# A four-layer kernel on one core: layer 0's modulations by column tiles, biases off TensorE, fused weights moved, y's first half taken later by ScalarE

## The chip, the cores and the metric

The kernel runs on one core of a Trainium2 chip. The metric is the device time of one execution in microseconds; lower is better. Before the change the median of three executions is 1902.47 us (1902.10 to 1903.45).

## The reference

Two sequences (2 x 1024 tokens x 256 channels, float32) go through four layers that are modulated by a vector of 512 numbers each. Cut to what matters:

```python
# layer 0: linear attention, 8 heads
xn = _ln(x, ln_w, ln_b)
q = softmax((xn @ Wq + bq).reshape(b, t, h, dh), axis=-1)
k = softmax((xn @ Wk + bk + mask).reshape(b, t, h, dh), axis=1)
v = ((xn @ Wv + bv) * src_mask).reshape(b, t, h, dh)
y = q @ (k^T v)                               # per head
scale, shift = split(silu(emb) @ W_emb + b_emb)
x = x + silu(_ln(y) * (1 + scale) + shift) @ W_out + b_out
# layer 1: tokens permuted, a Mamba block with 512 channels, 16 states
shift, scale, gate = split(silu(c) @ W_ada + b_ada)
h = (_layernorm(x) * (1 + scale) + shift)[:, perm]
def step(hst, inp):
    dA = exp(dt_t[:, :, None] * A)
    hst = hst * dA + (dt_t * x_t)[:, :, None] * B_t[:, None, :]
    y = einsum('bds,bs->bd', hst, C_t)
x = x + gate * ((y + xm * D) * silu(z) @ W_out)[:, inv_perm]
# layer 2: two such scans, forward and over the flipped sequence
mz = _ln(x_ssm) @ Wz.T + bz
z1 = _ssm(mz @ Wc1.T + bc1, ...);  z2 = flip(_ssm(flip(mz @ Wc2.T + bc2), ...))
out = (silu(mx) * z1 + silu(mx) * z2) @ Wf.T + bf + skip
# layer 3: softmax attention, 16 heads, then a modulated output as in layer 0
```

## The kernel before

**One program per engine.** Each engine runs a list of instructions written out in its own order (functions ending in `_sp` for SyncE, which starts the transfers, `_p` for GpSimd, `_t` for TensorE, `_s` for ScalarE, `_v` for VectorE). `w.wait_ge` makes an engine wait for a semaphore's value, and the instruction waits in order: what stands behind it on the engine waits too. `up(key)` names an event, `at(key)` is what others wait for. The eight PSUM banks are handed out in a ring: `take` waits until the bank's last reader has called `banks.give`.

**Layer 0** goes over 16 tiles of 128 tokens, in pairs. `first_t` projects q and v of a tile into one bank (bias matmul of three bf16 rows at line 440, two k-steps at 442) and transposes exp(k) (448). `first_s` copies v and exp(k) out, `first_v` reduces each q head's maximum (573), subtracts it and, one pair later, sums and normalises. Then TensorE forms attention (458), y, and between these the modulations: silu(c) times a weight matrix. `column_mods_t` (284) does that for values needed along partitions, as 16 accumulated narrow products with one or two columns, `row_mods_t` (320) for values needed along rows. Transposes (243) and the output projection (265) end it. The middle of layer 1's head gathers permuted rows from memory.

**Fused weights.** Layer 2 needs only Wz.Wc1 and Wz.Wc2 with their biases Wc.bz. `fuse_t(n)` makes both halves m = 0, 1 of matrix n (1069) and its bias (1074); it stands in the inputs of run one (n = 0) and of run two (n = 1). `fuse_s` (1080) copies the halves out. SyncE loads the second matrix after the first has been fused, `wzc1`, ahead of the C rows of run one in its queue.

**Six runs of scans.** A run is one sequence through one selective scan (layer 1, sequence 0 and 1; then layer 2, forward and backward for each sequence). `run_t`, `run_s`, `run_v`, `run_p` and `run_sp` work it off together. A run has 128 units: (half of 512 tokens) x (16 states) x (4 blocks of 128 channels). For a unit ScalarE makes the decay exp(dt A) (945), TensorE forms u = dt x B in PSUM three units ahead (854 with a diagonal of B that ScalarE spreads, 929, or 860 by transposing what ScalarE scaled, 922), VectorE scans (1014), ScalarE keeps the carry for the second half (937). GpSimd multiplies two units at once by a row of C that SyncE has loaded into all partitions (1037, loads at 815). TensorE adds these products up in four PSUM banks, transposed back to tokens (879). After 64 units the first half's y must be taken out of these banks before the second half's first product can be added. `take_s` and `take_v` do that, one bank of four each:

```python
        def by_scalar(r, p, j):
            return r.n < 2 and (p == 0 or j >= 2)
```

So in the runs with r.n = 0 or 1 (one, two, three and five) ScalarE takes the whole first half, and the last two banks of the second. In the backward ones (r.n = 2: four and six) VectorE takes all and adds it to the forward y (832). The take stands at unit `TAKEN_AT` = 71. At a run's end `turn_back_t` (1047) transposes y to channels, `turn_back_v` (1054) multiplies by the gates; in backward runs `open_gates_s` (1298), a SILU over 2 x 2048 elements, makes these gates just before, given to `run_s` as `early`. The start of a run (`inputs_t` and others, 672 and 691) prepares what the units need: ScalarE scales transposed inputs (749) and copies them (753), VectorE forms dt x (786).

## Time and profile before

| | before |
|---|---|
| median of three executions | 1902.47 us |
| profiled execution | 1901.27 us |
| its span (first to last instruction) | 1899.5 us |
| TensorE matmuls busy | 1816.6 us, 96% |
| VectorE busy | 1593.3 us, 84% |
| ScalarE busy | 1427.9 us, 75% |
| GpSimd busy | 1091.9 us, 57% |
| mean granted TensorE clock | 0.987 |

The busy shares are means over stages with different limits. The runs take from about 195 to 1399 us of the span; a little under 200 us lie before them and 500 behind (layer 3 mostly). A row of a timeline gives its start, the time to its end, engine, line, operation, output and inputs with shapes, and how many instructions it holds; in brackets stands the idle time of the engine before it and whose event ended it.

### The profile page before, as it was taken

To read this page: it belongs to the slowest core of one execution; us is meant where nothing else is said; L and a number is where in the kernel's file an instruction comes from. 1 tells how busy PE (TensorE), PEld (TensorE's weight loads), DVE (VectorE), ACT (ScalarE), POOL (GpSimd) and SP (SyncE) were. 2 spreads that over 40 slices of the span, in tenths; PEclk is the share of its full clock that TensorE was granted. 3 is DMA by queue.
4 is the path that set the end of the run, shared out by engine and by line. 5 is a ranking of instruction groups with operands and counts; after the bars stand their busy time and mean duration, and the time that the engine had idled before them with its cause. 6 is when DMAs were issued, how large, how long until landed. Compare 5 with 4: busy or idle time off the path is not lost.

```text
span 1899.5 us, 32305 instructions
## 1 busy us (share of the span) xinstructions
PE 1816.6 (96%) x12120; PEld 1309.2 (69%) x12120; DVE 1593.3 (84%) x2109; ACT 1427.9 (75%) x2669; POOL 1091.9 (57%) x615
## 2 busy tenths in 40 slices
PE   7999899998999999999999999999999999999997
PEld 3664899848997599959985799789974333322333
DVE  6566899578998699989995999799988888898772
ACT  3426999369993899799973999799955677776665
POOL 3022799438994499949990799679955400003000
PEclk9989899999999999999999999999999999999998
DMA  5032211121111112101110111121101111111101
GB/s 207 1 114 76 67 57 59 43 65 38 59 57 38 48 58 59 53 24 57 56 45 2 40 57 57 30 67 57 59 21 38 38 28 37 33 38 28 33 18 42
DMA packets 57546, 95.16 MB, mean 50 GB/s; under 512 B 14951, under 2 KB 23559, under 8 KB 55982
## 3 DMA queue, kind: packets, MB, share of 16 engines
q1 hardware_dynamic: 55854, 88.90, 15.5%
q0 software_dynamic: 1536, 4.20, 0.7%
q8 instruction: 96, 1.57, 0.3%
q14 instruction: 60, 0.49, 0.1%
HBM read 73.55 MB, written 6.91 MB: 42 GB/s over the span
## 4 chain that ended last, share of the span: by engine, by line
PE 51%; POOL 21%; issue 11%; ACT 10%; DVE 6%; SPq 1%; DMA 0%; DVEq 0%; ACTq 0%; POOLq 0%
POOL A L1037 20%; PE PS L256 8%; PE PS L1622 6%; PE PS L1574 6%; PE PS L879 5%; PE PS L1781 5%; PE PS L854 4%; PE PS L265 4%; PE PS L860 2%; ACT A L945 2%; PE PS L442 2%; DVE A L1587 1%; ACT A L922 1%; PE PS L243 1%; PE PS L1456 1%
## 5 line engine op out<-in xcount | busy, mean ns | idle before, releaser
L1037 POOL TENSOR_TENSOR A<-A 128x1024 f32<-128x1024 f32 x384 | 896.2, 2397 | 39.6 <-DVE A L1014 25.8
L945 ACT ACTIVATE A<-A,negA 128x512 f32<-128x512 f32 x768 | 547.6, 716 | 33.7 <-DVE A L1014 23.9
L1014 DVE TENSOR_TENSOR_SCAN A<-A,PS 128x512 f32<-128x512 f32 x384 | 434.7, 1199 | 27.4 <-PE PS L860 16.2
L1014 DVE TENSOR_TENSOR_SCAN A<-A,small,PS 128x512 f32<-128x512 f32 x384 | 451.2, 1256 | 5.6 <-ACT A L945 5.6
L879 PE MATMUL PS<-ident,A 128*128 128x128 f32 x3072 | 408.5, 275 | 23.9 <-ACT A L753 13.4
L854 PE MATMUL PS<-A 128*128 128x128 f32 x3072 | 392.6, 277 | 1.5 <-ACT A L929 1.2
L879 PEld LDWEIGHTS PS<-ident,A 128*128 128x128 f32 x3072 | 351.7, 142 | 34.0 <-ACT A L753 15.8
L854 PEld LDWEIGHTS PS<-A 128*128 128x128 f32 x3072 | 368.8, 192 | 5.5 <-DVE A L1014 2.8
L1587 DVE TENSOR_REDUCE A<-PS 128x1 f32<-128x512 f32 x512 | 319.7, 680 | 38.9 <-PE PS L1574 37.6
L1816 ACT ACTIVATE A<-PS 128x512 f32<-128x512 f32 x512 | 269.2, 604 | 106.6 <-PE PS L1781 106.3
L922 ACT ACTIVATE A<-A,small 128x512 f32<-128x512 f32 x320 | 228.7, 715 | 7.3 <-PE PS L860 7.2
L860 PE MATMUL PS<-ident,A 128*128 128x128 f32 x1360 | 197.3, 278 | 6.4 <-ACT A L753 3.0
L256 PE MATMUL PS<-A,W 128*128 128x512 f32 (+1 forms) x416 | 184.9, 598 | 3.3 <-DVE A L780 2.9
L1781 PE MATMUL PS<-A 102*128 102x512 bf16 x480 | 178.9, 381 | 7.0 <-ACT A L1816 5.1
L1574 PE MATMUL PS<-A 99*128 99x512 bf16 x480 | 179.8, 382 | 4.2 <-DVE A L1587 2.7
L1552 POOL CAST W<-W 128x32 bf16<-128x32 f32 x32 | 6.7, 209 | 303.6 <-DVE W L1545 303.6
L860 PEld LDWEIGHTS PS<-ident,A 128*128 128x128 f32 x1360 | 158.1, 142 | 15.2 <-DVE A L1014 4.9
L230 POOL TENSOR_TENSOR RS<-VE,HALF 128x8 f32<-128x8 f32 (+1 forms) x15 | 26.8, 1785 | 214.9 <-DVE VE L225 214.8
L929 ACT ACTIVATE A<-ident,small 128x128 f32<-128x128 f32 x384 | 149.1, 395 | 0.8 <-PE PS L854 0.8
L1574 PEld LDWEIGHTS PS<-A 99*128 99x128 bf16 x480 | 46.6, 97 | 146.1 <-DVE A L1587 108.1
L256 PEld LDWEIGHTS PS<-A,W 128*128 128x128 f32 (+1 forms) x416 | 75.1, 185 | 102.7 <-issue 91.6
L1622 PE MATMUL PS<-A,W 128*32 128x512 f32 x1024 | 136.5, 604 | 0.0
(195 smaller groups left out, 1827.7 us busy)
## 6 DMA issues: line engine op xcount, KB each, us to landing
A<-scrc SPq DMA_DIRECT2D x192, 256.0 KB, 3.1
A<-A SPq DMA_DIRECT2D x360, 32.0 KB
scr<-A SPq DMA_DIRECT2D x4, 1024.0 KB, 5.2
W<-in_wa SPq DMA_DIRECT2D x2, 1536.0 KB, 10.6
X<-in_x SPq DMA_DIRECT2D x4, 512.0 KB, 5.5
scr<-W SPq DMA_DIRECT2D x128, 1.5 KB
out<-X SPq DMA_DIRECT2D x4, 512.0 KB, 3.0
W<-in_w SPq DMA_DIRECT2D x1, 1984.0 KB
```

The costliest lines, as they stand in the source:

```text
L256: t = e.matmul(o[0:M, :], wt(k, m), act_in(k), start=k == 0, stop=k == nk - 1)
L854: t = e.matmul(o[:, j * 128:(j + 1) * 128], r.DUT[:, 4 * ci + j, dt * 128:(dt + 1) * 128], DB[k // 2 % 2][:, j, :], start=True, stop=True)
L860: t = e.transpose(o[:, j * 128:(j + 1) * 128], r.G[(2 * k + j) % 6][:, dt * 128:(dt + 1) * 128], ident[:, :])
L879: t = e.matmul(PS[:, j, dt * 128:(dt + 1) * 128], r.H[pair % HS][:, dt % 2, j * 128:(j + 1) * 128], ident[:, :], start=open_y(ci, j), stop ...
L945: e.activation(A_B[i % 4], r.DT[:, dt, ci * 512:(ci + 1) * 512], ACT.Exp, scale=negA[:, r.n, dt * 16 + s:dt * 16 + s + 1]).then_inc(*decay ...
L1014: e.tensor_tensor_scan(h, a, u, init, ALU.mult, ALU.add).then_inc(*scanned.up((q, i)))
L1037: e.tensor_tensor(h, h, CB[k % 2].unsqueeze(1).broadcast_to([128, 2, 512]), ALU.mult).then_inc(*weighed.up((q, pair)))
L1574: e.matmul(o, SQ[j][0:99, nt * 128:(nt + 1) * 128], SK3[j][0:99, c * 512:(c + 1) * 512], start=True, stop=True).then_inc(*pe.up(("trial", ...
L1587: e.tensor_reduce(NM[:, k % 2, q:q + 1], bank(("trial", k, nt, c)), AX.X, ALU.max, negate=True).then_inc(*dve.up(("trial", k, nt, c)))
L1622: t = e.matmul(PV[32 * q:32 * q + 32, u % 2, :], V[:, tile * 272 + 17 * h:tile * 272 + 17 * h + 32], PX[mt % 4][j][:, c * 512:(c + 1) * 51 ...
L1781: e.matmul(o, SK3[sl][0:102, mt * 128:(mt + 1) * 128], SQ[sl][0:102, c * 512:(c + 1) * 512], start=True, stop=True).then_inc(*pe.up(("scor ...
L1816: e.activation(PX[mt % 4][j][:, c * 512:(c + 1) * 512], bank(key), ACT.Exp).then_inc(*act.up(("weights", u, mt, j, c)))
```

## The change

It does seven things. (1) The bias of q and v no longer is a matmul: SyncE loads it into all partitions (`bias_qv`), VectorE adds q's in an instruction per tile, GpSimd adds v's (times the mask) to the copied v. (2) Column and row modulations are formed as a 32-column stationary operand (silu(c) padded by zeros, `sc32`) against 512 columns of weights, the four k-blocks in four column tiles of the array. ScalarE copies the parts, and short matmuls with `sel` add the four blocks up. (3) The biases of the fused weights take the same way (`bias_parts_t`). (4) Three of the four fused products stand at the end of layer 0; the last stands in run one's inputs. SyncE loads these weights in `first_sp`, and nothing of them in `layer1_sp`. (5) ScalarE pulls two transposed inputs of the second half at units 6 and 7, not 9 and 10. (6) ScalarE takes y's first half at the point of unit 75 and not 72, in all runs, and TensorE forms u of one unit before it adds up there. (7) In backward runs ScalarE takes the first half, and banks 2 and 3 of the second, into a buffer of its own (`r.DUT`), and `turn_back_t` adds it by a second transpose into the same bank. Line numbers move: what stood at 1014 (scan), 1037 (GpSimd) and 945 (decay) now stands at 1101, 1124 and 1030.

```diff
+        def parts_t(e, w, key, lhs, rhs):
+
+            o = take(w, (key, "parts"))
+            for n, (at, wt) in enumerate(rhs):
                 for k in range(4):
-                    t = e.matmul(o[:, 2 * m:2 * m + 2], wt[:, k, at:at + 128], sc[:, k, :], start=k == 0, stop=k == 3)
-            t.then_inc(*pe.up(("mods", layer)))
+                    t = e.matmul(o[32 * k:32 * k + 32, at[0]:at[1]], lhs[:, k, :], wt(k), start=True, stop=True, tile_position=(0, 32 * k),
+                                 skip_group_check=True)
+            t.then_inc(*pe.up((key, "parts")))
+
+        def parts_s(e, w, key):
+            w.wait_ge(*pe.at((key, "parts")))
+            e.activation(parts_of(key), bank((key, "parts")), ACT.Copy).then_inc(*act.up((key, "parts")))
+            banks.give((key, "parts"), act.now())
+
+        def column_sums_t(e, w, key, chunks):
+            o = take(w, key)
+            w.wait_ge(*act.at((key, "parts")))
+            for m, at in chunks:
+                t = e.matmul(o[:, 2 * m:2 * m + 2], parts_of(key)[:, at:at + 128], sel, start=True, stop=True)
+            t.then_inc(*pe.up(key))
...
@@ first_p
+            for i in range(0, NT, 2):
+                w.wait_ge(*act.at(("v", i + 1)))
+                e.tensor_tensor(V0[:, i:i + 2, :], V0[:, i:i + 2, :], BVM[:, i:i + 2, :], ALU.add).then_inc(*pool.up(("v", i)))
@@ first_t, loop over pairs of tiles
-                    e.matmul(o, ones3[0:3, :], ROW3[0:3, 0:512], start=True, stop=False)
                     for k in range(2):
-                        t = e.matmul(o, XN[:, k, (i + j) * 128:(i + j + 1) * 128], w0[:, 0:3:2, k, :], start=False, stop=k == 1)
+                        t = e.matmul(o, XN[:, k, (i + j) * 128:(i + j + 1) * 128], w0[:, 0:3:2, k, :], start=k == 0, stop=k == 1)
@@ first_t, end
+            for n in range(2):
+                bias_parts_t(e, w, n)
+            for n in range(2):
+                row_sums_t(e, w, n)
+            column_sums_t(e, w, ("mods", 2), orders(2))
+            for n, m in FUSED[0:3]:
+                fuse_t(e, w, n, m)
+            for n in range(2):
+                column_sums_t(e, w, ("bzc", n), [(j, 128 * j) for j in range(4)])
@@ first_v
-                    e.tensor_reduce(m, b3, AX.X, ALU.max, negate=True).then_inc(*dve.up(("qmax", j)))
+                    e.tensor_tensor(Q0[:, j, :], bank(("qv", j))[:, 0:256], BQ, ALU.add).then_inc(*dve.up())
+                    banks.give(("qv", j), dve.now())
                     w.wait_ge(*dve.now())
-                    e.tensor_tensor(q3, b3, m.unsqueeze(2).broadcast_to([128, 8, 32]), ALU.add).then_inc(*dve.up(("qsub", j)))
-                    banks.give(("qv", j), dve.now())
+                    e.tensor_reduce(m, q3, AX.X, ALU.max, negate=True).then_inc(*dve.up(("qmax", j)))
+                    w.wait_ge(*dve.now())
+                    e.tensor_tensor(q3, q3, m.unsqueeze(2).broadcast_to([128, 8, 32]), ALU.add).then_inc(*dve.up(("qsub", j)))
@@ taking y
         def by_scalar(r, p, j):
-            return r.n < 2 and (p == 0 or j >= 2)
+            return p == 0 or j >= 2
+
+        def taken_to(r, p, j, y):
+
+            i = 4 * r.order[p] + j
+            return r.DUT[:, i, :] if r.n == 2 else y(i)
@@ run_t
-                if dt % 2 and i >= 7:
+                late = i == 2 * (PAIRS_N // 2) + 7
+                if dt % 2 and i >= 7 and not late:
                     add_up((i - 7) // 2)
                 form_u(i + 3)
+                if late:
+                    add_up((i - 7) // 2)
@@ run_s
+            if q == 0:
+                fuse_s(e, w, *FUSED[3])
             for j in range(4):
                 if not first_state(r, j)[2]:
                     scale_du_s(e, w, r, j)
...
-                if i == TAKEN_AT + 1:
+                if i == TAKEN_AT + 4:
...
-                if i in (9, 10):
-                    copy_du_s(e, w, r, 1, i - 7)
+                if i in (6, 7):
+                    copy_du_s(e, w, r, 1, i - 4)
@@ turn_back_t
-                    t = e.transpose(o[:, j * 128:(j + 1) * 128], y(4 * c + j)[:, m * 128:(m + 1) * 128], ident[:, :])
+                    parts = [y(4 * c + j)] + ([taken_to(r, p, j, y)] if r.n == 2 and by_scalar(r, p, j) else [])
+                    for n, part in enumerate(parts):
+                        t = e.matmul(o[:, j * 128:(j + 1) * 128], part[:, m * 128:(m + 1) * 128], ident[:, :], start=n == 0, stop=True,
+                                     is_transpose=True, skip_group_check=True)
@@ layer1_sp
             store_c_sp(e, w, runs[0])
-            w.wait_ge(*act.at(("wzc", 0)))
-            w.wait_ge(*dve.at(("bzc", 0)))
-            e.dma_start(w2all, T["wzc"][:, 3072:5120]).then_inc(*transfer("wzc1").up(0))
             run_sp(e, w, runs[0])
```

Three places show how the instructions move. A row gives line, operation, output and inputs by buffer name, size and count.

TensorE's queue at the end of layer 0, from the output projection of sequence 0 (265, now 267) on. Before, the modulations are narrow products (284) and row products (320):

```order
L265 MATMUL PS<-A 128x256 x16
L284 MATMUL PS<-sc,W 128x2 x16
L320 MATMUL PS<-W,sc 2x256 x4
L243 MATMUL PS<-ident,A 128x128 x16
L265 MATMUL PS<-A 128x256 x16
L320 MATMUL PS<-W,sc 2x256 x4
L320 MATMUL PS<-W,sc 2x512 x4
L284 MATMUL PS<-sc,A 128x2 x16
L243 MATMUL PS<-ident,A 128x128 x16
```

Now (293 are the column tiles, 309 and 348 the sums, 1167 the three fused products):

```order
L267 MATMUL PS<-A 128x256 x16
L293 MATMUL PS<-W,small 32x512 x4
L293 MATMUL PS<-A,small 32x512 x4
L245 MATMUL PS<-ident,A 128x128 x16
L309 MATMUL PS<-small,A 128x2 x4
L267 MATMUL PS<-A 128x256 x16
L293 MATMUL PS<-A 32x512 x8
L348 MATMUL PS<-A,small 2x512 x2
L309 MATMUL PS<-small,A 128x2 x4
L1167 MATMUL PS<-A 128x512 x12
L309 MATMUL PS<-small,A 128x2 x8
L245 MATMUL PS<-ident,A 128x128 x16
```

Between the second projection and layer 1's first transposes (243, now 245) stand the fused products now.

ScalarE's queue at the end of run four, before:

```order
L929 ACTIVATE A<-ident,small 128x128
L945 ACTIVATE A<-A,negA 128x512 x8
L1298 ACT_TABLE_LOAD
L1298 ACTIVATE A<-A 128x4x512 x2
L250 ACTIVATE A<-PS,COL 128x512 x4
```

And now:

```order
L1014 ACTIVATE A<-ident,small 128x128
L1030 ACTIVATE A<-A,negA 128x512 x8
L908 ACTIVATE A<-PS 128x512 x2
L1391 ACT_TABLE_LOAD
L1391 ACTIVATE A<-A 128x4x512 x2
L252 ACTIVATE A<-PS,COL 128x512 x4
```

Two copies of y's banks (908), which wait for the last addition, stand ahead of the gates (1391).

ScalarE's queue at the start of run one, from the first decays (945, now 1030), before and then now:

```order
L945 ACTIVATE A<-A,negA 128x512 x4
L749 ACTIVATE A<-PS,small 128x512 x4
L753 ACTIVATE A<-PS 128x512 x4
L929 ACTIVATE A<-ident,small 128x128 x4
L1080 ACTIVATE W<-PS 128x512 x2
L922 ACTIVATE A<-A,small 128x512
```

```order
L1030 ACTIVATE A<-A,negA 128x512 x4
L1172 ACTIVATE W<-PS 128x512
L826 ACTIVATE A<-PS,small 128x512 x4
L830 ACTIVATE A<-PS 128x512 x4
L1014 ACTIVATE A<-ident,small 128x128 x4
L1007 ACTIVATE A<-A,small 128x512
```

One copy of fused weights (1172) stands ahead of the scalings (826) in place of two (1080) behind the spreads.

## Rows read from the trace of the kernel before

**Rows 1.** Timeline of VectorE, middle of run one.

```profile
284.89 1.28 DVE L1014 TENSOR_TENSOR_SCAN A<-A,small,PS 128x512 f32<-128x512 f32 x1 [1.39 <-ACT A L945]
```

**Rows 2.** Timeline of GpSimd across the same moment.

```profile
267.78 23.37 POOL L1037 TENSOR_TENSOR A<-A 128x1024 f32<-128x1024 f32 x10
```

**Rows 3.** GpSimd's waits (us, count, longest), 436 to 590 and 841 to 990.

```profile
POOL A L1037 <- DVE A L1014: 5.3, 3, 4.2
...
POOL A L1037 <- DVE A L1014: 6.3, 3, 5.8
```

**Rows 4.** Timeline of TensorE, layer 0.

```profile
50.93 0.38 PE L440 MATMUL PS<-ROW,ones 3*128 3x512 bf16 x1
51.24 1.99 PE L442 MATMUL PS<-A 128*128 128x512 f32 x4
...
74.09 5.27 PE L458 MATMUL PS<-A 128*128 128x128 f32 x32
...
80.95 3.74 PE L458 MATMUL PS<-A 128*128 128x128 f32 x32
...
94.49 2.93 PE L243 MATMUL PS<-ident,A 128*128 128x128 f32 x16 [0.91 <-ACT negA L521]
...
98.58 7.17 PE L265 MATMUL PS<-A 128*128 128x256 f32 x32 [1.16 <-ACT A L250]
```

**Rows 5.** Timeline of VectorE, two tiles of layer 0's loop.

```profile
46.27 0.42 DVE L573 TENSOR_REDUCE small<-PS 128x8 f32<-128x256 f32 x1 [1.35 <-ACT A L504]
...
48.94 0.42 DVE L573 TENSOR_REDUCE small<-PS 128x8 f32<-128x256 f32 x1 [0.18 <-ACT A L504]
```

**Rows 6.** Groups by line, 0 to 215 us: busy us, mean ns, idle before.

```profile
L320 PE MATMUL PS<-W,sc 128*2 128x256 f32 (+1 forms) x24 | 8.9, 532 | 0.0
...
L284 PE MATMUL PS<-sc,W 128*128 128x2 f32 x64 | 8.5, 268 | 0.0
```

**Rows 7.** Timeline of TensorE, layer 3.

```profile
1500.64 1.07 PE L1622 MATMUL PS<-A,W 128*32 128x512 f32 x8
```

**Rows 8.** Timeline of TensorE, start of run one.

```profile
179.40 7.06 PE L1069 MATMUL PS<-W 128*128 128x512 f32 x16
186.30 3.63 PE L1074 MATMUL PS<-COL,W 128*128 128x2 f32 x32
```

**Rows 9.** Windows: PE, PEld, DVE, ACT, POOL busy (instructions), granted clock, DMA share, GB/s.

```profile
132.00:138.00 6.00, 6.00 (x23) 4.86 (x24) 4.15 (x19) 3.10 (x4) 0.51 (x1) 0.50 0.01 5
```

**Rows 10.** Timeline of ScalarE, start of run one.

```profile
190.92 0.69 ACT L749 ACTIVATE A<-PS,small 128x512 f32<-128x512 f32 x1 [3.55 <-PE PS L672]
...
197.09 1.10 ACT L1080 ACTIVATE W<-PS 128x512 f32<-128x512 f32 x2
```

**Rows 11.** Timeline of SyncE, loads of C's rows, start of run one.

```profile
198.59 15.19 SPq L815 DMA_DIRECT2D A<-scrc  x4
```

**Rows 12.** Timeline of GpSimd, start of run one.

```profile
204.13 11.62 POOL L1037 TENSOR_TENSOR A<-A 128x1024 f32<-128x1024 f32 x5 [8.93 <-ACT small L937]
```

**Rows 13.** Timeline of ScalarE, start of run two.

```profile
427.72 2.42 ACT L749 ACTIVATE A<-PS,small 128x512 f32<-128x512 f32 x4 [3.08 <-PE PS L672]
```

**Rows 14.** Timeline of VectorE, end of run four.

```profile
991.97 2.48 DVE L1054 TENSOR_TENSOR A<-PS,A 128x512 f32<-128x512 f32 x4 [1.86 <-PE PS L1047]
```

**Rows 15.** Timeline of ScalarE, end of run four.

```profile
986.20 1.28 ACT L1298 ACT_TABLE_LOAD   x1
987.49 3.71 ACT L1298 ACTIVATE A<-A 128x2048 f32<-128x2048 f32 x2
```

**Rows 16.** Timeline of TensorE, end of run four.

```profile
991.26 1.91 PE L1047 MATMUL PS<-ident,A 128*128 128x128 f32 x16
...
996.89 1.64 PE L1047 MATMUL PS<-ident,A 128*128 128x128 f32 x13 [0.27 <-DVE A L832]
```

**Rows 17.** Timeline of VectorE, start of run one.

```profile
178.74 2.29 DVE L786 TENSOR_TENSOR A<-A 128x2048 f32<-128x2048 f32 x1 [4.17 <-ACT A L720]
...
186.03 3.16 DVE L786 TENSOR_TENSOR A<-A 128x2048 f32<-128x2048 f32 x1
```

## What the change is predicted to do

> **What bounds the kernel now.** I read the page's slices first, then the timelines of single engines. The span has three kinds of stretch, and an edit is worth something only by the limit of its own stretch.
>
> Six runs of 64 pairs of scans. In the middle of the first run VectorE stands still for 1.39 us at the turn to the second half [rows 1], yet GpSimd's ten multiplications across that moment take 23.37 us with no pause, 2.34 us each [rows 2]. So GpSimd sets the pace from its first pair to its last; VectorE only has to stay ahead. A run ends when GpSimd has done 64 pairs, and gets shorter only by an earlier first pair or by fewer pauses of GpSimd. The waits of GpSimd on VectorE come to 5.3 us in the second run, of which 4.2 is the wait before the first pair, and to 6.3 with 5.8 before the first in the fourth [rows 3]: 1.1 and 0.5 us of pauses are left.
>
> Layer 0 and the head of layer 1 (to about 168 us). TensorE works nearly without a pause, and what it has to do is the time.
>
> Starts and ends of runs: chains of one engine after another.
>
> **The change, part by part.**
>
> 1. Biases of q and v off TensorE. The bias matmul takes 51.24 - 50.93 = 0.31 us of TensorE's time per tile [rows 4]; 16 tiles, 5.0 us. VectorE gets an addition per tile; its neighbours of that shape take 0.42 us, 0.46 with the dependency, 0.92 for a pair of tiles. It idles 1.35 + 0.18 = 1.53 us in each pair [rows 5], and a pair gets 0.62 shorter on TensorE: 1.53 - 0.92 - 0.62 is nothing, so VectorE goes from idle to level with TensorE. I count the whole 5.0 for TensorE, since banks let it run more than two pairs ahead. GpSimd's additions to v are needed only by the attention matmuls after the loop.
>
> 2. Column and row modulations by column tiles. Before: 64 narrow matmul instructions take 8.5 us, 0.133 each, so the three sets of 32 take 12.8; the row ones take 8.9 [rows 6]; together 21.7, of which I take 0.5 off because modelled ends overlap the next start: 21.2. After: a group of four column tiles, 512 wide, is 8 instructions and takes 1.0 us where the kernel already does that [rows 7]. Five groups are 5.0. Three column sums are 8 narrow instructions each, 0.95, so 2.85. Two row sums are 2 instructions of 512 columns each, at the 0.44 of the 16 wide ones in [rows 8]: 1.8. That is 9.7, so 11.5 saved. ScalarE's copies of the parts (0.6 each) fall where it idles.
>
> 3. Fusions. All of Wz.Wc was done at the starts of runs one and two: two products in 7.06 us and the bias in 3.63 [rows 8], in each. Now three of four products stand at the end of layer 0 (10.3 us) with both biases (2 groups, 2.0, and 16 narrow instructions, 1.8): 14.1 us added there. They could hide a wait for the gathered rows, but TensorE has had none there.
>
> 4. Clock. After the long stretches of narrow matmuls TensorE's granted clock is 0.50, its 1.2 GHz level [rows 9]. The first attention product takes 5.27 us at it and 3.74 as the second one at the full level [rows 4]: 1.5 lost. The 6 us at 132 to 138 [rows 9] do the work of 3: 3.0 lost. The narrow stretches shrink from 32 instructions to 8, so I expect both back, 4.5. Bounds: 0 and 4.5.
>
> TensorE also waits 0.91 before the transposes of normalised y and 1.16 before the output projection [rows 4]; parts now stand in these places: 2.0. Front: 5.0 + 11.5 - 14.1 + 4.5 + 2.0 = **8.9 us** earlier at the first run. Bounds 3 and 10.
>
> 5. Start of run one. TensorE fuses until 189.8, while ScalarE idles 3.55 us for the transposed inputs; two copies of fused weights (1.0 us) come later [rows 8, 10]. Left: one product (3.5 us), hidden behind VectorE's input of run one, and one copy, placed ahead. ScalarE: 3.55, about 0.5 of small waits between the four scalings (an estimate), and 1.0 for the copies less 0.6 for the one that stays: 4.5 earlier. But GpSimd's first pair waits longer than ScalarE explains: SyncE issues the first row of C at 198.59 only, behind the load of the second half of the weights, which waits for that fusion [rows 11], and GpSimd starts at 204.13 [rows 12]. That load is gone from the queue, so the pair can start after ScalarE's first carry, which comes about a pair's work of ScalarE earlier; I take 2.2 for it, just under GpSimd's pace of 2.34 [rows 2]: 204.1 - 2.2 - 4.5 = 197.4. **6.7 us**. Bounds: 4.5 and 6.9.
>
> 6. Start of run two. ScalarE's wait of 3.08 us for the transposes [rows 13] goes, and its two copies (1.0): 4.0. VectorE is then the next to be late. The two pulls of inputs moved from units 9 and 10 to 6 and 7 end TensorE's waits in units 9 to 13, and with them the 1.1 us of GpSimd's pauses: **5.1**. Bounds 3 and 6. Runs four and six: 0.5 each, **1.0**. Runs three and five have no such pause: 0.
>
> 7. y's first half three units later. VectorE's 1.39 us vanish in four runs, and four additions (2.48 us, the shape of the gatings in [rows 14]) in two. GpSimd never stopped there [rows 2], so I count **0**; the cover is its lead of about one pair of work. If the cover were gone: 4 x 1.4 + 2 x 2.5 = 10.6 us.
>
> 8. Backward y. ScalarE now takes y tiles 2 and 3 at the end of runs four and six, and `run_s` puts these copies ahead of `open_gates_s`, which was free to run before the end. Before: the table load at 986.20 and the two SILUs are done by 991.2 [rows 15]; VectorE's four gatings start at 991.97 [rows 14]. After, in the times of that run: the last 32 transposes of the first half (16 before, 1.91 us with its modelled end [rows 16], some 1.75 from start to start) take 3.5 us, 991.26 to 994.76; the last addition (0.62 as a gating [rows 14], with its hand-overs) 1.0, 995.8; ScalarE's two copies of the last bank, 996.6; table load 1.28, 997.9; first SILU 1.86, 999.8 [rows 15]; four gatings 2.48, 1002.2; VectorE's two copies, then TensorE's 24 transposes. Before, the fourth addition let TensorE go at 996.89 with 13 transposes left, 1.6 us [rows 16], so it ended at 998.5. Now VectorE's second addition is done at 1003.5, 22 or 23 transposes are left, 2.7 us: 1006.2. **7.7 us** later, and the output projection stands behind it in TensorE's queue. Twice: **+15.4**. Bounds 6 and 8.5 for each. This is the largest single term.
>
> Sum: -8.9 - 6.7 - 5.1 - 1.0 + 15.4 = -6.3 on the profiled execution's 1901.3, 1895.0; the median of the runs is 1.2 above that execution, so **1896 us**.
>
> **Two rules against the change.** VectorE's product over 2048 elements takes 2.29 us alone and 3.16 while GpSimd multiplies [rows 17]. In the loop of layer 0 GpSimd will add v's bias while VectorE subtracts and normalises; VectorE has no slack there by step 1. If each pair of tiles loses 0.9 us so, eight pairs lose 7, of which TensorE's lead of some two pairs hides a part: the front gives 4 in place of 8.9. The Trainium skill (SBUF - State Buffer, on the shared port pair) says that a VectorE instruction with two SBUF inputs and a GpSimd instruction that reads SBUF shut each other out for the whole instruction; by that rule the trace agrees, and the sum would be near 1901.
>
> The groups of four column tiles take 1.0 us between other matmuls [rows 7], so a switch costs little. The Trainium skill (TensorEngine Tiling (Array Packing), Key Properties) says that changing the tiling mode drains TensorE; no row prices the drain apart.
>
> **Rivals.**
> - The late gate is right, the front gives less (the lock above, the low clock staying, or the gathered rows late by what TensorE gained): 4 to 6 us of the 8.9 gone, 1900 to 1902, no change. For: VectorE has no slack. Against: the attention products come later. 0.20.
> - VectorE, not GpSimd, is the pace after all, so step 7 pays 10: 1886. Against it: [rows 2]. 0.08.
> - The gate costs nothing (the SILUs are hidden): 1881. It would need ScalarE to open gates before its copies, and the order says no. 0.04.
> - Slower: GpSimd's first pair in runs one and two hangs on VectorE's second input product and its own scaling of the skip, and not on ScalarE or the row of C. Then steps 5 and 6 give 0 to 2 of 11.8 and the late gates decide: 1906. It decides from the point at which less than 6 of the 11.8 come. Against it: GpSimd idles 8.93 us before the first pair [rows 12]. 0.06.
> - Forecast: 1892 to 1900, 0.62.
>
> **Numbers.** About 0.2% (3.8 us) is what a measurement of this kernel can tell from no change, so faster means under 1898.7. Of the forecast's 0.62 about four fifths lie there; with 0.08 and 0.04 and some of the first rival, faster 0.66. Same: the rest of the forecast and most of the first rival, 0.27. Slower 0.07. The range, 1888 to 1902, leaves out the fast rivals and the slow one.
>
> **What would show it.** Per tile 1.9 us on TensorE in layer 0's loop; groups of 8 instructions at 1.0; no half clock before 190 us; the first conv projection some 9 us earlier; GpSimd's first pair near 188 in run one; VectorE's pause in mid-run gone, GpSimd's row unchanged; and at the end of runs four and six a table load after the last addition, with VectorE idle some 8 us before its gatings. Wrong if that idle time is absent, if GpSimd pauses in mid-run, or if a wait for gathered rows stands before the first transposes of layer 1.

## The result

The changed kernel takes 1911.42 us (median of 7 executions, 1909.74 to 1915.74) where the kernel before took 1902.11 (7 executions, 1898.73 to 1903.45). The ratio is 1.0057, 95% interval 1.0044 to 1.007: slower by 9 us between the medians, outside the predicted range and on the other side of no change. The profiled execution of the changed kernel takes 1915.28 us with a span of 1913.4, 13.9 longer than the span before; it is one of three executions near 1915, at a granted clock of 0.983, while the other four lie between 1909.7 and 1911.4 at 0.985 to 0.986.

The busy times of the page hardly explain that. TensorE does less and is granted less of its clock (0.983, 0.987 before):

```profile
PE 1803.4 (94%) x12076; PEld 1299.4 (68%) x12076; DVE 1601.0 (84%) x2114; ACT 1435.6 (75%) x2688; POOL 1110.8 (58%) x627
```

What explains it is a list of milestones, read from the timelines of TensorE and GpSimd of the two profiled executions (us). A part of the change is what its stretch gains or loses between two of them.

| milestone | before | after | after - before | this stretch | predicted |
|---|---|---|---|---|---|
| first attention product, layer 0 | 74.09 | 63.90 | -10.2 | -10.2 | |
| first projection, layer 1 | 136.32 | 134.61 | -1.7 | +8.5 | -8.9 for both |
| GpSimd's last pair ends, run one | 354.00 | 345.00 | -9.0 | -7.3 | -6.7 |
| the same, run two | 589.40 | 577.91 | -11.5 | -2.5 | -5.1 |
| the same, run three | 808.85 | 798.38 | -10.5 | +1.0 | 0 |
| the same, run four | 992.60 | 981.47 | -11.1 | -0.7 | -0.5 |
| first output projection after run four | 998.67 | 999.36 | +0.7 | +11.8 | +7.7 |
| GpSimd's last pair ends, run five | 1215.05 | 1216.85 | +1.8 | +1.1 | 0 |
| the same, run six | 1398.86 | 1399.95 | +1.1 | -0.7 | -0.5 |
| first output projection after run six | 1404.90 | 1417.98 | +13.1 | +12.0 | +7.7 |
| end of the span | 1899.49 | 1913.38 | +13.9 | +0.8 | 0 |

**Layer 0.** TensorE goes through the loop faster than was predicted. A pair of tiles took 4.90 us from start to start:

```profile
55.82 0.39 PE L440 MATMUL PS<-ROW,ones 3*128 3x512 bf16 x1
...
60.72 0.38 PE L440 MATMUL PS<-ROW,ones 3*128 3x512 bf16 x1
```

It takes 3.87 now (the prediction takes 0.62 off a pair, the rows show 1.03):

```profile
55.35 3.60 PE L486 MATMUL PS<-A 128*128 128x512 f32 x8
...
59.22 3.60 PE L486 MATMUL PS<-A 128*128 128x512 f32 x8
```

So TensorE comes 10.2 us earlier to attention, and gives 8.7 of it back within 21 us. Its timeline from the last of layer 0's loop on:

```profile
63.90 3.82 PE L507 MATMUL PS<-A 128*128 128x128 f32 x32
67.56 1.40 PE L515 MATMUL PS<-ident,A 128*128 128x128 f32 x8
69.19 0.66 PE L515 MATMUL PS<-ident,A 128*128 128x128 f32 x4 [0.24 <-DVE A L647]
70.99 0.66 PE L515 MATMUL PS<-ident,A 128*128 128x128 f32 x4 [1.14 <-DVE A L647]
74.29 3.78 PE L507 MATMUL PS<-A 128*128 128x128 f32 x16 [2.64 <-ACT A L572]
79.38 3.78 PE L507 MATMUL PS<-A 128*128 128x128 f32 x16 [1.31 <-DVE MT L317]
...
134.61 31.14 PE L258 MATMUL PS<-A,W 128*128 128x512 f32 x72 [0.35 <-issue]
```

Where the second attention product had no wait before it and took 3.74 us [rows 4], it stands in two halves now, each of 3.78 us behind a wait; TensorE's granted clock is at the half level from 72.9 to 83.1 us. VectorE has no idle time at all from 40 to 58 us and is the one that is late. Its timeline shows one instruction twice as long for every other tile, and four much too long at the end:

```profile
64.87 0.98 DVE L652 TENSOR_TENSOR A<-A,small 128x256 f32<-128x256 f32 x1
...
66.67 0.42 DVE L652 TENSOR_TENSOR A<-A,small 128x256 f32<-128x256 f32 x1
...
71.42 1.66 DVE L652 TENSOR_TENSOR A<-A,small 128x256 f32<-128x256 f32 x1
...
74.00 1.84 DVE L664 TENSOR_TENSOR A<-A,small 128x512 f32<-128x512 f32 x1
...
76.97 1.65 DVE L664 TENSOR_TENSOR A<-A,small 128x512 f32<-128x512 f32 x1
...
79.35 1.49 DVE L320 TENSOR_SCALAR MT<-MT 128x4 f32<-128x4 f32 x1
```

GpSimd's timeline has the counterpart: an addition to v beside the first, and from 70.28 on four additions of the output bias to x. Those stood at 21 us before; they have been queued behind the additions to v.

```profile
64.30 1.27 POOL L459 TENSOR_TENSOR A<-A 128x512 f32<-128x512 f32 x1 [3.49 <-ACT A L567]
69.05 1.27 POOL L459 TENSOR_TENSOR A<-A 128x512 f32<-128x512 f32 x1 [3.48 <-ACT A L567]
70.28 10.54 POOL L463 TENSOR_TENSOR X<-X,A 128x1024 f32<-128x1024 f32 x4
```

**The runs.** GpSimd's first pair of run one starts at 194.35 where it started at 204.13 [rows 12], and then GpSimd has a pause that it did not have, between its first and its second pair:

```profile
194.35 2.37 POOL L1124 TENSOR_TENSOR A<-A 128x1024 f32<-128x1024 f32 x1 [1.92 <-issue]
198.25 2.37 POOL L1124 TENSOR_TENSOR A<-A 128x1024 f32<-128x1024 f32 x1 [1.53 <-ACT small L1022]
```

It stands in all six runs, 1.5 to 1.7 us in four and 0.8 in the backward ones, and waits for the carry (1022). In mid-run nothing has changed for GpSimd, as in [rows 2]: eleven pairs in 25.69 us, 2.34 each.

```profile
261.16 25.69 POOL L1124 TENSOR_TENSOR A<-A 128x1024 f32<-128x1024 f32 x11
```

VectorE's pause there has not gone, as was predicted, but shrunk from 1.39 to 0.82 us, and it waits for TensorE's addition now; runs four and six, which had none, have the same 0.82.

```profile
276.28 9.55 DVE L1101 TENSOR_TENSOR_SCAN A<-A,small,PS 128x512 f32<-128x512 f32 x8 [0.82 <-PE PS L961]
```

**The ends of runs four and six** are the largest loss. TensorE, then VectorE, then ScalarE, end of run four:

```profile
980.98 5.25 PE L1136 MATMUL PS<-ident,A 128*128 128x128 f32 x32
986.06 1.04 PE L961 MATMUL PS<-ident,A 128*128 128x128 f32 x8
994.61 4.61 PE L1136 MATMUL PS<-ident,A 128*128 128x128 f32 x24 [7.51 <-DVE A L914]
999.15 0.28 PE L194 MATMUL PS<-ROW,ones 3*128 3x256 bf16 x1
```

```profile
991.47 2.49 DVE L1144 TENSOR_TENSOR A<-PS,A 128x512 f32<-128x512 f32 x4 [15.49 <-ACT A L1391]
993.87 1.27 DVE L914 TENSOR_TENSOR A<-A,PS 128x512 f32<-128x512 f32 x2
```

```profile
987.13 1.08 ACT L908 ACTIVATE A<-PS 128x512 f32<-128x512 f32 x2 [15.08 <-PE PS L961]
988.24 1.28 ACT L1391 ACT_TABLE_LOAD   x1
989.53 3.71 ACT L1391 ACTIVATE A<-A 128x2048 f32<-128x2048 f32 x2
```

The reader sees the chain as predicted: last addition, two copies, table load, one SILU, four gatings, two additions of VectorE, 24 transposes. In the windows view (busy time and count of PE, PEld, DVE, ACT and POOL, then the granted clock) one also sees what the sum left out, a lowered clock. It is at the half level twice, from 977.4 to 984.2 us, which begins before the last pair ends and ahead of TensorE's long wait, and from 991.0 to 997.9, which begins in that wait:

```profile
978.00:986.00 8.00, 7.22 (x43) 6.82 (x42) 0.00 (x0) 0.00 (x0) 3.47 (x2) 0.61 0.00 0
986.00:994.00 8.00, 1.10 (x11) 0.86 (x8) 2.53 (x5) 6.08 (x5) 0.00 (x0) 0.82 0.00 0
994.00:1000.00 6.00, 5.27 (x28) 4.64 (x29) 3.93 (x7) 0.00 (x0) 0.00 (x0) 0.68 0.00 0
```

### The profile page after: what moved, and what is told of

It is laid out like the page before. It is cut to its first block, busy times and chain, and to the rows that moved or that the text cites. A ratio compares the mean times of both kernels' runs of the same rounds, so it can differ in the third digit from the quotient of the medians.

```text
span 1913.4 us, 32264 instructions
## 1 busy us (share of the span) xinstructions
PE 1803.4 (94%) x12076; PEld 1299.4 (68%) x12076; DVE 1601.0 (84%) x2114; ACT 1435.6 (75%) x2688; POOL 1110.8 (58%) x627
## 4 chain that ended last, share of the span: by engine, by line
PE 38%; ACT 27%; POOL 18%; issue 8%; DVE 7%; SPq 1%; DMA 0%; DVEq 0%; POOLq 0%; ACTq 0%
POOL A L1124 17%; ACT A L1030 12%; PE PS L258 8%; PE PS L1715 6%; PE PS L1667 6%; ACT A L1007 5%; PE PS L1874 5%; PE PS L267 4%; ACT A L1014 3%; DVE A L1680 1%; PE PS L1136 1%; ACT small L1022 1%; PE PS L245 1%; PE PS L749 1%; PE PS L1549 1%
## 5 line engine op out<-in xcount | busy, mean ns | idle before, releaser
L936 PE MATMUL PS<-A 128*128 128x128 f32 x3072 | 388.3, 276 | 0.3
L1014 ACT ACTIVATE A<-ident,small 128x128 f32<-128x128 f32 x384 | 150.1, 397 | 0.0
## 6 DMA issues: line engine op xcount, KB each, us to landing
W<-in_wa SPq DMA_DIRECT2D x2, 1536.0 KB, 10.5
```

The lines of the kernel that those rows point to most:

```text
L936: t = e.matmul(o[:, j * 128:(j + 1) * 128], r.DUT[:, 4 * ci + j, dt * 128:(dt + 1) * 128], DB[k // 2 % 2][:, j, :], start=True, stop=True)
```

## The experiments

Executions of one kernel differ by up to 6 us; so stretches of the profiled executions decide where single microseconds matter, and medians where the sum does. In what follows, "the stretch" is from the end of GpSimd's last pair to the first output projection's matmul with the weights, after run four and after run six. It is 6.1 and 6.0 us before the change, 17.9 and 18.0 after.

The clock moves this stretch too. Four of the kernels below leave that chain as the change has it: it takes 16.2 and 16.2 us (pulls at 9 and 10), 16.7 and 16.4 (no additions to v), 16.2 and 18.4 (additions to x first), 17.9 and 18.1 (biases on TensorE). Where it is 16.2 to 16.7 there is no half clock ahead of the wait, and the 32 transposes take 3.66 us, but the 24 behind it are slow all the same. TensorE at the end of run four, pulls at 9 and 10:

```profile
977.16 3.66 PE L1136 MATMUL PS<-ident,A 128*128 128x128 f32 x32
...
989.20 5.37 PE L1136 MATMUL PS<-ident,A 128*128 128x128 f32 x24 [7.51 <-DVE A L914]
```

### The gates ahead of the copies

```diff
-                run_s(e, w, two, y2, lambda part: gates_s(e, w, b, GATES[PARTS[part]]))
-                open_gates_s(e, w, b)
+                run_s(e, w, two, y2, lambda part: gates_s(e, w, b, GATES[PARTS[part]]), lambda: open_gates_s(e, w, b))
```

> The changed kernel, with ScalarE's opening of the gates placed ahead of its last two copies of y in runs four and six; all else as changed. Measured on the changed kernel: 17.7 us from the end of GpSimd's last pair to the first output projection in run four (5.9 before the change), 17.8 in run six (5.8). Theory: the gates behind the copies are the larger part of this. Then the table load and both SILUs vanish under GpSimd's last pairs, VectorE's first gating starts when the 32 transposes are done (about 4.7 after GpSimd's end and not 10.0), and the stretch falls to 11 to 12 us; twice, 12 us, 1899. Rival: the doubled transposes at the low clock and the last addition set it, the gates are nearly hidden; the stretch stays over 15, 1906 or more.

Measured: 1896.59 us (1893.26 to 1899.38), ratio to before 0.9973 (0.9962 to 0.9984). The stretches are 7.4 and 9.1 us. The theory holds and was too modest. The timeline at the end of run four has no low clock in it, and the 23 transposes take 2.73 us:

```profile
987.08 2.73 PE L1136 MATMUL PS<-ident,A 128*128 128x128 f32 x23 [0.27 <-DVE A L914]
```

The same view of windows says so for the whole end:

```profile
980.00:992.00 12.00, 10.70 (x82) 9.47 (x82) 8.09 (x15) 1.09 (x2) 2.52 (x2) 1.00 0.00 1
```

So most of the 11.8 and 12.0 us lost hangs on the order of two statements on ScalarE, and on the low clock that comes with the wait. Like is to be compared with like here. In run four neither this kernel nor the one with 16.2 us has half clock ahead of the last transposes: 8.8 us. In run six this kernel and the changed one both have it (the 32 transposes take 4.43 and 4.25 us): 18.0 - 9.1 = 9.0. Of what remains, 1.4 us is the price of the doubled transposes and of the copies, and in run six another 1.6 is the half clock at 1388.2 to 1391.6 us, which stands there without any long wait.

### Backward y by VectorE

```diff
         def by_scalar(r, p, j):
-            return p == 0 or j >= 2
+            return r.n < 2 and (p == 0 or j >= 2)
```

> The changed kernel with VectorE taking and adding backward y again, one transpose per block, as before the change; the late point of the take and all else stay. Theory: the whole loss of the change sits in the two ends of the backward runs, so these stretches go back to 5.9 us from 17.7, 23.7 us in all: 1888, faster than the kernel before by some 14. The four additions of VectorE in mid-run (2.5 us) cost GpSimd nothing, since its lead there was two pairs. Rival: with the late take VectorE's additions in mid-run reach GpSimd, which then pauses up to 2.5 us in each backward run: 1890 to 1893.

Measured: 1892.75 us (1890.34 to 1896.11), ratio 0.9954 (0.9941 to 0.9968). Both stretches are 6.1 us again, the span 1890.7, 22.7 below the changed one. GpSimd's stretches in runs four and six are 150.3 and 150.4 us (150.4 and 150.3 with ScalarE taking y): the additions of VectorE in mid-run cost nothing, and the rival falls. (The time alone would not decide it: it lies in the rival's 1890 to 1893.) The time is 4.8 us above the expected 1888: the expectation took 23.7 from the median, 1911.4, while the profiled execution in which the 23.7 were read is itself 3.9 longer than that median.

### The wait alone, in the kernel before

```diff
                 run_s(e, w, two, y2, lambda part: gates_s(e, w, b, GATES[PARTS[part]]))
+                w.wait_ge(*added.at((two.q, PAIRS_N - 1)))
                 open_gates_s(e, w, b)
```

> The kernel before the change with one wait added: ScalarE opens the gates of runs four and six only after TensorE's last addition of the run, which is where its two copies now make it wait. No copy, no second transposes. Theory: this wait alone is most of the loss. From the end of GpSimd's last pair to the first output projection 6.0 us before; now the last addition ends at 1.4, table load and first SILU take 3.2, four gatings 2.5, VectorE's four additions 2.5 and the transposes behind them 1.6 at the full clock and 3.2 at the low one: 11.5 to 13.5; twice, and the time is 1914 to 1917. Rival: the doubled transposes and ScalarE's copies are most of it and the wait alone costs less than 3 us each: 1908 or less.

Measured: 1914.74 us (1912.59 to 1915.37), ratio 1.0081 (1.0063 to 1.0098). Both stretches are 11.6 us, 5.6 more than before. One wait of ScalarE makes the kernel before slower by more than the whole change does (a ratio of 1.0081 against 1.0057). TensorE's timeline shows the cost behind the wait:

```profile
996.22 4.83 PE L1047 MATMUL PS<-ident,A 128*128 128x128 f32 x16 [5.11 <-DVE A L832]
1000.98 0.39 PE L195 MATMUL PS<-ROW,ones 3*128 3x256 bf16 x1
```

Sixteen transposes span 4.83 us, where 13 took 1.64 [rows 16]; the granted clock is at the half level from 995.7 to 1002.5, after TensorE had waited 5.11. The profiled executions account for 11 of the 15 us between the medians; the other 4 are scatter, since the profiled execution here is 2.2 us under its median and the one before the change 1.5 over the median taken beside this one (1899.75).

In the changed kernel the wait is worth more than these 5.6, because copies and 24 transposes at the half clock, not 16, stand behind it: 8.8 to 9.0.

### GpSimd's additions to x first

```diff
+            w.wait_ge(*transfer("bias_o").at(0))
+            w.wait_ge(*dve.at((("ln0", 1), NT - 1)))
+            for i in range(0, NT, 4):
+                e.tensor_tensor(X[:, i:i + 4, :], X[:, i:i + 4, :], BO.unsqueeze(1).broadcast_to([128, 4, D]), ALU.add).then_inc(*pool.up("x_bias"))
             e.memset(bz32, 0.0).then_inc(*pool.up())
...
-            for i in range(0, NT, 4):
-                e.tensor_tensor(X[:, i:i + 4, :], X[:, i:i + 4, :], BO.unsqueeze(1).broadcast_to([128, 4, D]), ALU.add).then_inc(*pool.up("x_bias"))
```

> The changed kernel with GpSimd's four additions of the output bias to x (10.5 us, at 70 to 81 us) moved ahead of its work on v's bias, where they stood before the change. Theory: there they shut out VectorE's products of two SBUF operands: its four instructions at 71.4, 74.0, 77.0 and 79.4 take 1.66, 1.84, 1.65 and 1.49 us, where their like takes 0.42, 0.69, 0.69 and 0.17. They fall to that, VectorE is done with the modulations 4.5 us earlier, and layer 1's first projections start about 4 us earlier than at 134.6: 1907. Rival: TensorE's waits at 67 to 82 us come from the low clock and the matmuls alone: less than 1 us.

Measured: 1908.85 us (1907.39 to 1911.85), ratio 1.0039 (1.0025 to 1.0053). Layer 1's first projection starts at 131.86, 2.75 us earlier. VectorE is done with the modulations at 77.9 and not at 81.4, and the product that took 1.84 us takes its own time again, while one per pair still takes 0.97:

```profile
66.03 0.97 DVE L652 TENSOR_TENSOR A<-A,small 128x256 f32<-128x256 f32 x1
...
73.92 0.69 DVE L664 TENSOR_TENSOR A<-A,small 128x512 f32<-128x512 f32 x1
```

The mechanism is shown, the expected 4 us were too many: VectorE's gain is 3.5, and TensorE still had the half clock from 72.4 to 79.3 us.

### No additions to v

```diff
-            for i in range(0, NT, 2):
-                w.wait_ge(*act.at(("v", i + 1)))
-                e.tensor_tensor(V0[:, i:i + 2, :], V0[:, i:i + 2, :], BVM[:, i:i + 2, :], ALU.add).then_inc(*pool.up(("v", i)))
```

> The changed kernel without GpSimd's eight additions of v's bias in layer 0's loop (v's bias is left out of the result); VectorE's additions of q's bias stay. Theory: each of these eight shuts out one of VectorE's products of two SBUF operands, which takes 0.97 us where the same instruction of the next tile takes 0.42, and VectorE, without a pause there, sets the pair at 4.76 us. Without them 4.2, eight times 0.55; GpSimd's additions to x come early too and no longer meet the end of the loop. Layer 1's first projection starts at 128 to 129 us, from 134.6 (131.9 with only the additions to x moved). Rival: VectorE's extra instruction per tile is the whole of it and the shared access costs nothing: the pair stays at 4.7 and the projection starts at 131.9.

This kernel leaves v's bias out, and GpSimd's additions to x come early in it too. Measured: 1906.30 us (1905.27 to 1910.84), ratio 1.0032 (1.0018 to 1.0046). The projection starts at 128.78. A pair takes 4.20 us on VectorE (51.27 to 55.47), and every product of the loop takes 0.42, except the two that meet GpSimd's additions to x, which now run from 31.50 to 41:

```profile
36.30 2.46 DVE L648 TENSOR_TENSOR A<-A,small 128x256 f32<-128x256 f32 x1
...
39.58 1.67 DVE L648 TENSOR_TENSOR A<-A,small 128x256 f32<-128x256 f32 x1
...
66.52 0.43 DVE L648 TENSOR_TENSOR A<-A,small 128x256 f32<-128x256 f32 x1
```

The theory holds to 0.1 us per pair, the rival falls. With VectorE's extra instruction per tile still there, the projection starts 4.3 us earlier than with the biases on TensorE (133.05, next section): without GpSimd's reads most of the predicted 5.0 us would have arrived.

### The biases of q and v on TensorE

```diff
+                    e.matmul(o, ones3[0:3, :], ROW3[0:3, 0:512], start=True, stop=False)
...
-                    e.tensor_tensor(Q0[:, j, :], bank(("qv", j))[:, 0:256], BQ, ALU.add).then_inc(*dve.up())
```

VectorE's two other instructions per tile and GpSimd's queue in the loop are as before the change too.

> The changed kernel with the biases of q and v back on TensorE, as before the change; everything else as changed, backward y too. Theory: in layer 0's loop the change has swapped a pace of 4.90 us per pair set by TensorE for 4.76 set by VectorE, and has made the end of the loop late by GpSimd's additions to x. So the undo loses nothing: layer 1's first projection starts at 132 to 133, against 134.6 now, 2 us faster in all, 1909. Rival: the 5.0 us of TensorE's time are gained as predicted and the loss is elsewhere in the front (low clock, the fused products, the gathered rows): the projection starts at 138 to 140 and the time is 1915 or more.

Measured: 1912.44 us (1910.07 to 1913.05), ratio 1.0059 (1.0046 to 1.0073). The projection starts at 133.05, 1.6 us earlier than in the changed kernel, as expected; attention starts at 72.50, 8.6 later, and TensorE then has no wait there. The medians don't show the 1.6 us, the stretches do. So this part of the change gains nothing: TensorE comes 8.6 us earlier to attention by it, and spends all of that and 1.6 us more waiting for VectorE and at the half clock. Here there is no half clock before 186 us.

### The pulls at units 9 and 10

```diff
-                if i in (6, 7):
-                    copy_du_s(e, w, r, 1, i - 4)
+                if i in (9, 10):
+                    copy_du_s(e, w, r, 1, i - 7)
```

> The changed kernel with ScalarE's two pulls of inputs back at units 9 and 10. Theory: at units 6 and 7 they delay ScalarE's second carry, and this is the pause of 1.6 us (0.9 in runs four and six) that GpSimd has after its first pair in every run now. It goes, and the pauses among the pairs three to nine of runs one, two, four and six come back (1.0 to 1.3 us). GpSimd's stretch from first to last pair goes from 150.6 to 149.9 in run one, 150.7 to 151.3 in run two, 150.9 to 149.9 in runs three and five, 150.3 to 151.0 in runs four and six: 1 us faster in sum, 1910.5. Rival: the pause has another cause (the row of C, VectorE's scans) and stays; then the old pauses come on top: 4 to 5 us slower.

Measured: 1910.19 us (1908.29 to 1911.11), ratio 1.0043 (1.0029 to 1.0057), no difference that a median shows. GpSimd's stretches from first to last pair are 149.7, 150.7, 149.9, 151.0, 149.9 and 150.9 us, against 150.6, 150.7, 150.9, 150.4, 151.0 and 150.3: as expected but for run two, where the old pauses return only in part (0.24, 0.67 and 0.54 us). The pause behind the first pair is gone in run three, GpSimd's timeline:

```profile
644.80 4.70 POOL L1124 TENSOR_TENSOR A<-A 128x1024 f32<-128x1024 f32 x2 [4.08 <-DVE A L1101]
```

With the pulls at 6 and 7, ScalarE's timeline there reads as follows: it waits for the transposed inputs and pulls both before it reaches the carry (1022) that GpSimd waits for.

```profile
649.01 0.60 ACT L830 ACTIVATE A<-PS 128x512 f32<-128x512 f32 x1 [0.74 <-PE PS L749]
...
650.73 0.58 ACT L830 ACTIVATE A<-PS 128x512 f32<-128x512 f32 x1
651.21 0.20 ACT L1022 ACTIVATE small<-A 128x2 f32<-128x2 f32 x1
```

### The three together, and what is left

The first of two kernels puts backward y on VectorE, the pulls at 9 and 10 and the biases on TensorE; the second keeps the biases off TensorE but has the additions to x first.

> The changed kernel with three parts undone: backward y by VectorE, the biases of q and v on TensorE, the pulls of inputs at units 9 and 10. What is left of the change: column tiles, the moved fusions, the take at the later point. The theory adds the three: 1892.8 less 2 for the front less 3 for GpSimd's first pairs, 1887 to 1888. Rival: the parts hide one another and it stays at 1892.

> As the one before, but with the biases of q and v off TensorE as in the change and GpSimd's additions to x moved ahead of them. Theory: layer 1's first projection at 131.9, about as early as with the biases on TensorE; the same 1887 to 1888. Rival: the loop gains more this way, over 1 us between the two.

Measured: 1887.65 us (1887.25 to 1890.28), ratio 0.9934 (0.9921 to 0.9948), and 1888.08 us (1886.33 to 1888.44), ratio 0.9931 (0.9918 to 0.9945). The parts add up. Both are about 12 us faster than the kernel before (1900.01 beside them), and the medians do not tell them apart. What is left of the change, column tiles and moved fusions above all, is its gain, and it had been there all along; the two were not measured apart. In the profile of the first, 3.4 us are gained up to layer 1's first projection, 8.1 from there to GpSimd's first pair, and 3.5 from the end of run one to that of run two.

### The take at unit 72 again

```diff
-                late = i == 2 * (PAIRS_N // 2) + 7
+                late = False
...
-                if i == TAKEN_AT + 4:
+                if i == TAKEN_AT + 1:
```

This is done in the second of these two kernels.

> The kernel that measured 1888.1 (backward y by VectorE, additions to x first, pulls at units 9 and 10), and in it y's first half taken by ScalarE at unit 72 again and TensorE adding up there in the old order. Theory: VectorE's pause of 1.4 us in mid-run comes back in runs one, two, three and five, and GpSimd never shows it, since it lags VectorE by 2 to 3 us there. GpSimd's stretches stay within 0.3 us of 150.6, 150.0, 150.0, 151.2, 149.9 and 150.9, and the time at 1888. Rival: VectorE's pause comes through; 1.4 us more in each of four runs, 1893 to 1894.

Measured: 1887.90 us (1887.09 to 1890.60), ratio 0.9943 (0.9925 to 0.9961). GpSimd's stretches are 149.8, 150.0, 149.9, 151.2, 149.9 and 151.0 us; only run one differs by more than 0.3, and it is shorter with VectorE's pause than without (the other kernel had the half clock from 199 to 202 us). VectorE's pause is back, 1.03 us at 271 us and 1.4 in runs two, three and five, where it is 0.82 with the late take; GpSimd's ten pairs across it take 23.29 us:

```profile
271.46 14.21 DVE L1101 TENSOR_TENSOR_SCAN A<-A,small,PS 128x512 f32<-128x512 f32 x12 [1.03 <-ACT A L1030]
```

```profile
261.76 23.29 POOL L1124 TENSOR_TENSOR A<-A 128x1024 f32<-128x1024 f32 x10
```

### The pulls by the kind of run

```diff
-                if i in (9, 10):
-                    copy_du_s(e, w, r, 1, i - 7)
+                a = 6 if r.n == 2 else 9
+                if i in (a, a + 1):
+                    copy_du_s(e, w, r, 1, i - a + 2)
```

> The kernel that measured 1888.1 with the two pulls at units 6 and 7 in runs four and six alone, and at 9 and 10 in the others. Theory: runs four and six last 150.3 us on GpSimd with the early pulls and 151.0 with the late ones, the others 149.9 to 150.6 with the late ones and 150.6 to 150.9 with the early ones, so each gets its better place: 1.4 us less, 1886.7. Rival: the differences come from what precedes a run and not from the pulls: no change from 1888.1.

Measured: 1887.30 us (1884.22 to 1889.41), ratio 0.9935 (0.9921 to 0.9949). GpSimd's stretches are 149.8, 150.1, 149.9, 150.3, 149.9 and 150.4: each as expected. The gain of 0.8 us in run four arrives; the 0.6 of run six are lost at its end, where the stretch is 7.4 and not 6.1, with the half clock from 1385.1 to 1388.5 us. The median can't tell this kernel from the one that it came from.

## Why the prediction was wrong

It named the mechanisms and got the sum wrong: 15 us between 1896 and 1911.4. The steps in its order:

1. **Biases off TensorE, -5.0: this step failed.** It counted the whole gain of TensorE's time and left GpSimd's reads out of VectorE's period. Its estimate that VectorE would be "level with TensorE" was right by itself: it implies 4.3 us a pair, and without GpSimd's additions to v VectorE took 4.20. With them it took 4.76, and that was the pace; TensorE, with 3.87 of its own, ran ahead and then waited. Two things were not put in the sum. The exclusion of VectorE's products by GpSimd stood among the rules against the change at 0.9 us a pair (measured: 0.55, eight times; the projection comes 3.1 us earlier without it and without the half clock that stood there). And the additions to v were followed, but not what stood behind them in GpSimd's queue: the additions to x moved from 21 us to 70 us, into VectorE's last instructions (2.75 us). Measured, this part is 1.6 us slower than no change at all: 4.3 gained, 3.1 and 2.75 lost. On the rule of the Trainium skill (SBUF - State Buffer, on the shared port pair), which the prediction weighed, the trace agrees: VectorE's product took 0.97 us beside GpSimd's addition and 0.42 without.
2. **Column tiles, -11.5; fusions at the front, +14.1; clock, -4.5; waits, -2.0.** Together -3.9. With the biases back on TensorE the first projection starts at 133.05, 3.3 us earlier than before the change, so these held. The column tiles took 1.04 to 1.07 us a group, the three fused products 10.55. In the changed kernel itself the clock did not hold: the sign "no half clock before 190 us" failed at 72.9 us, among the waits of item 1.
3. **Start of run one, -6.7**: -7.3 measured, and the chain was right. That the two are so close is in part luck: the first pair came 8.1 us earlier against the first projection, over the bound of 6.9, and 0.8 went to the new pause. Of the 8.1, 1.1 is the clock of item 2, which the milestones put here (72 matmuls of the projections took 32.20 us before and 31.14 after).
4. **Start of run two, -5.1**: -2.5 measured. From VectorE's first input (409.12 before, 401.50 after) to the first pair the gain is 3.3 of the predicted 4.0, and 0.6 of the 1.1 in pauses arrived. The other 1.4 is lost where the step did not look, at the end of run one: the granted clock is at the half level from 342.5 to 345.9 us there. Of the eleven kernels with the fusion moved away, the six that have half clock at this place need 82.1 to 82.3 us from run one's last pair to run two's first, the five without it 80.8. That VectorE is "the next to be late" was right. The removed fusion let TensorE wait 6.61 us, and the inputs were then transposed at the half clock; from 411 to 425 us the granted clock is 0.63, where it was 1.00:

```profile
415.82 3.67 PE L749 MATMUL PS<-ident,A 128*128 128x128 f32 x16 [6.61 <-DVE A L857]
```

```profile
411.00:425.00 14.00, 7.92 (x39) 7.52 (x39) 13.90 (x11) 13.47 (x22) 8.57 (x3) 0.63 0.34 127
```

   But this low clock cost the run nothing: VectorE is busy 13.90 of these 14 us, and its scans follow its last input without a gap.

```profile
420.30 2.29 DVE L865 TENSOR_TENSOR A<-A 128x2048 f32<-128x2048 f32 x1
422.51 5.66 DVE L1101 TENSOR_TENSOR_SCAN A<-A,PS 128x512 f32<-128x512 f32 x5
```

   The earlier pulls, which were to end 1.1 us of pauses, also brought one of 1.5 to 1.7 behind the first pair (and so the 1.0 us lost in runs three and five each). It was said which pauses they end and not whom they make wait: the carry is the next thing on ScalarE's queue.
5. **The take three units later, 0**: right, in both kinds of run, though VectorE's pause only shrank to 0.82 us.
6. **Backward y, +7.7 each**: the chain was right link by link, and 11.8 and 12.0 were measured. The term was undersized by the clock, in two places. The 24 transposes at the end took 4.61 and 5.76 us and not 2.7: the half clock begins in the wait that the step itself predicted, in each of the ten ends of runs with that wait (five kernels), and that was not followed. Where this is the only half clock, the stretch is 16.2 us; with the transposes at 2.7 it would be 13.5, which is 7.5 over the kernel before, against the predicted 7.7. The other place lies ahead of the wait, and not every execution has it: in the profiled one the 32 transposes took 5.25 and 4.25 us and not 3.5. What lowers the clock there stays open.

Of the rivals the first came true in its mechanism (the front gives less), together with a larger late gate than either had. The slow rival, which hung on GpSimd's first pair, did not. No case let two terms be wrong in the same direction, and the range ended at 1902.

One thing is open: which stretches make the profiled execution of the changed kernel 4 us longer than its median was not seen, since there is no profile of a shorter one. The half clock ahead of the two waits, worth about 1.7 us each, is a candidate and not shown.

## What to carry to other kernels

When work moves from a busy engine to a half idle one, compute the period of the loop on the receiving engine with everything it gets, contention included, and take the larger of the two; an engine that comes out level has nothing left for a contention of 0.55 us a pair. Follow the queue of every engine that receives work past the new instruction: what stood behind it (additions to x, a carry, the opening of gates) moves as well, and lands beside other things. A predicted wait of TensorE as long as those here (5.1 to 7.5 us) wants the half clock for what follows it in the sum, and a table load or an activation that needs no late input belongs ahead of the copy that does.

## What the runs showed of the hardware

- GpSimd's addition of 128x512 (1.27 us) lengthened VectorE's 128x256 product of two SBUF operands from 0.42 to 0.97 us, and its 128x1024 ones (2.3 to 2.8 us) to between 1.66 and 2.46. In the changed kernel the lengthened 128x256 product ended 0.28 us behind GpSimd's addition, beside both sizes. Additions that read one operand from PSUM, and reductions, kept their 0.42 beside them.
- In waits of 5.1 to 7.5 us, or within 0.1 us of their end, TensorE's granted clock fell to the half level every time (23 such waits in the twelve profiles that have one): 24 transposes took 4.61 and 5.76 us behind them, and 23 took 2.73 where the wait had been 0.8.
- Less work on TensorE lowered its clock where it had been cover: without the fusion ahead of run two its granted clock was 0.63 from 411 to 425 us, in which VectorE and not TensorE set the pace.
- A table load and a SILU moved ahead of two copies by order alone shortened the end of a run by 8.8 to 9.0 us.
